# Plain cross-attention: scores in four bursts of four blocks, two of each burst copied half by ScalarE and half by VectorE

## The reference, cut to what matters

```python
q = (x @ Wq).reshape(B, N, HEADS, DIM_HEAD)        # B 2, N 256, HEADS 8, DIM_HEAD 64
k = (context @ Wk).reshape(B, M, HEADS, DIM_HEAD)  # M 4096
v = (context @ Wv).reshape(B, M, HEADS, DIM_HEAD)
sim = jnp.einsum('bihd,bjhd->bhij', q, k) * SCALE
attn = jax.nn.softmax(sim, axis=-1)
out = jnp.einsum('bhij,bjhd->bihd', attn, v).reshape(B, N, INNER)
return out @ Wo + bo
```

## Time and profile before

| | |
|---|---|
| median of three runs | 1962.62 us |
| the profiled execution: its time, its span | 1959.22 us, 1957.3 us |
| TensorE busy, of the span | 1825.8 us (93%) |
| VectorE | 1570.7 us (80%) |
| ScalarE | 857.4 us (44%) |
| GpSimd | 923.8 us (47%) |
| plain stage on TensorE | from 12.6 us to about 542 us |
| one sweep of the plain stage | 62.8 us |

### The profile page before, as it was taken

How to read it: one execution, slowest core, us unless ns; L and a number is a source line. 1 busy time by engine, 2 the same in 40 slices (tenths; PEclk the granted TensorE clock), 3 DMA queues, 4 the chain that set the end, 5 groups by cost and what they waited for, 6 DMA issues and landing times. The chain is left out here.

```text
span 1957.3 us, 44087 instructions
## 1 busy us (share of the span) xinstructions
PE 1825.8 (93%) x17242; PEld 1268.8 (65%) x17242; DVE 1570.7 (80%) x2178; ACT 857.4 (44%) x1173; POOL 923.8 (47%) x438
## 2 busy tenths in 40 slices
PE   7999999999877979899999999999999999998737
PEld 4667666667636868866666676666666666666526
DVE  4666766677777756699999999999999999999783
ACT  3666666676531135433434344334434344343401
POOL 0346655575560034116655575556655575556300
PEclk9999999999988889999999999999999999999757
DMA  3000210000030033000000000120000000000100
GB/s 137 10 15 0 66 48 13 1 12 10 7 141 1 2 149 95 29 9 2 13 13 13 8 5 13 46 68 0 13 13 13 6 7 13 13 8 1 50 0 11
DMA packets 27771, 52.77 MB, mean 27 GB/s; under 512 B 4259, under 2 KB 15284, under 8 KB 27188
## 3 DMA queue, kind: packets, MB, share of 16 engines
q1 hardware_dynamic: 27232, 51.57, 7.9%
q10 hardware_dynamic: 468, 0.16, 0.0%
HBM read 51.20 MB, written 0.52 MB: 26 GB/s over the span
## 5 line engine op out<-in xcount | busy, mean ns | idle before, releaser
L351 POOL TENSOR_TENSOR biased_sums<-biased_sums,biased_scores 128x1024 f32<-128x1024 f32 x216 | 512.4, 2372 | 138.8 <-ACT biased_scores L651 119.0
L717 DVE TENSOR_TENSOR biased_scores<-ps,bias 128x1024 f32<-128x1024 f32 x256 | 313.5, 1224 | 35.3 <-PE ps L439 33.9
L731 DVE TENSOR_TENSOR ps<-ps,biased_scores 128x512 f32<-128x512 f32 x480 | 336.5, 701 | 4.1
L738 DVE TENSOR_TENSOR biased_scores<-biased_scores,ps 128x1024 f32<-128x1024 f32 x256 | 307.5, 1221 | 3.8 <-PE ps L496 3.1
L651 ACT ACTIVATE biased_scores<-biased_scores 128x1024 f32<-128x1024 f32 x256 | 262.9, 1052 | 97.9 <-DVE biased_scores L738 95.7
L351 POOL TENSOR_TENSOR plain_sums<-plain_sums,plain_scores 128x1024 f32<-128x1024 f32 x104 | 246.5, 2370 | 60.7 <-ACT plain_scores L651 50.3
L731 DVE TENSOR_TENSOR ps<-ps,plain_scores 128x512 f32<-128x512 f32 x240 | 167.3, 697 | 118.2 <-ACT plain_scores L634 113.3
L439 PE MATMUL ps<-biased_queries,keys_again 64*128 64x256 f32 x2048 | 256.7, 390 | 3.6 <-DVE biased_scores L717 2.8
L386 PE MATMUL ps<-weights_again,context_again 128*64 128x128 f32 x4096 | 248.7, 275 | 0.0
L451 PE MATMUL ps<-biased_scores,biased_values 128*64 128x256 f32 x2048 | 245.4, 382 | 3.5 <-ACT biased_scores L651 3.2
L386 PEld LDWEIGHTS ps<-weights_again,context_again 128*64 128x64 f32 x4096 | 229.3, 138 | 28.7 <-issue 17.9
(11 more groups left out here) (407 smaller groups left out, 2238.1 us busy)
## 6 DMA issues: line engine op xcount, KB each, us to landing
moe_w<-in_moe_w SPq DMA_DIRECT2D x32, 256.0 KB, 2.7
weights_again<-in_wqkv SPq DMA_DIRECT2D x45, 128.0 KB, 2.2
context<-in_ctx_t SPq DMA_DIRECT2D x4, 1024.0 KB, 7.1
context_again<-in_ctx_t SPq DMA_DIRECT2D x4, 1024.0 KB, 7.8
bias<-in_fside SPq DMA_DIRECT2D x1, 4096.0 KB, 15.4
biased_w_out<-in_w_out SPq DMA_DIRECT2D x16, 256.0 KB, 2.6
context<-in_ctx_t SPq DMA_DIRECT2D x2, 1536.0 KB, 9.7
context_again<-in_ctx_t SPq DMA_DIRECT2D x2, 1536.0 KB, 9.7
```

Source lines behind the costliest of these rows:

```text
L351: pool.tensor_tensor(both(SUM[:, :, :, :]), both((E[:, 0] if kp == 1 else SUM)[:, :, :, :]), both(E[:, kp, :, :, :]), ALU.add).then_inc(su ...
L717: dve.tensor_tensor(E[:, kp, :, :, :].rearrange("p (h t) n j -> p h t (n j)", h=2), scores_bank(kp).rearrange("p (h t n) -> p h t n", h=2, ...
L731: ins = dve.tensor_tensor(to, highest, E[:, kp, :, n, :], ALU.max)
L738: dve.tensor_tensor(at, at, c.ps[:, LOWER, :].rearrange("p (a j) -> p a j", a=HQ).unsqueeze(2) .to_broadcast([P, HQ, 2, P]), ALU.add).then ...
```

## The change

In the plain stage a sweep that makes scores is now four bursts: W, V, W, V, then four score blocks in a row, then one K piece. Before, a pair of score blocks stood in each of the eight groups. The fourth key piece (K4) moves behind the sums at the sweep's end. In each burst the first two score blocks are copied half by ScalarE (banks of the first head) and half by VectorE (`half_out`); the other two are copied whole by ScalarE, as before. The third and fourth block of a burst wait for both halves. The biased stage keeps its order.

```diff
+BURST_PIECES = [("V", 0), ("V", 1), ("K", 0), ("V", 2), ("V", 3), ("K", 1), ("V", 4), ("V", 5), ("K", 2), ("V", 6),
+                ("V", 7), ("K", 3), ("K", 4), ("K", 5), ("K", 6), ("K", 7)]
...
+        def in_halves(kp):
+            return not biased and kp % BURST < 2
...
                     if kp >= 2:
                         pe.wait_ge(scores_kept, NP * p + kp - 1)
+                        if in_halves(kp - 2):
+                            pe.wait_ge(halves_kept, halves_count(p, kp - 2))
...
+                def bursts(m, attending):
+                    for d in range(NP // BURST):
+                        for g in (2 * d, 2 * d + 1):
+                            if attending:
+                                weigh(m, g)
+                            piece(m, ("V", g))
+                        for i in range(BURST):
+                            scores(m + 1, BURST * d + i)
+                        piece(m, ("K", d))
...
                     if more_keys:
+                        if not biased:
+                            piece(m, ("K", 4))
                         piece(m, ("K", 5))
...
+                    if in_halves(kp):
+                        act.activation(E[:, kp, 0:2, :, :].rearrange("p a n j -> p (a n j)"),
+                                       c.ps[:, 2 * (kp % 2), :], ACT.Copy).then_inc(scores_kept, 1)
...
+                def bursts(m, attending):
+                    for d in range(NP // BURST):
+                        later = range(BURST * d + AHEAD, BURST * d + AHEAD + BURST) if attending and d < NP // BURST - 1 else ()
+                        for kp in later[0:1]:
+                            exponential(m, kp)
+                        piece_out(m, ("V", 2 * d))
+                        for kp in later[1:3]:
+                            exponential(m, kp)
+                        piece_out(m, ("V", 2 * d + 1))
+                        for i in range(BURST):
+                            scores_out(m + 1, BURST * d + i, attending)
+                        piece_out(m, ("K", d))
+                        for kp in later[3:4]:
+                            exponential(m, kp)
...
+                def half_out(p, kp, attending):
+                    dve.wait_ge(scores_done, NP * p + kp + 1)
+                    if attending:
+                        dve.wait_ge(summed, NP * (p - 1) + max(kp, 1))
+                    dve.tensor_copy(E[:, kp, 2:4, :, :].rearrange("p a n j -> p (a n j)"),
+                                    c.ps[:, 2 * (kp % 2) + 1, :]).then_inc(halves_kept, 1)
...
+                def bursts(m, attending):
+                    for d in range(NP // BURST):
+                        for kp in range(BURST * d, BURST * (d + 1)):
+                            if attending and kp + AHEAD < NP:
+                                lower(m, kp + AHEAD)
+                            if d > 0:
+                                peak(m + 1, kp - BURST, 0)
+                                peak(m + 1, kp - BURST, 1)
+                        for i in range(2):
+                            half_out(m + 1, BURST * d + i, attending)
+                    for kp in range(NP - BURST, NP - 1):
+                        peak(m + 1, kp, 0)
+                        peak(m + 1, kp, 1)
```

More of the change, by code:

```diff
@@ L202, in cross_attention @@
     LAST_SUMS, LATE_SUMS = 8, 12
-    V_PIECES = [piece for piece in PIECES if piece[0] == "V"]
+    BURST = 4
+    ALL_PIECES = PIECES if biased else BURST_PIECES
+    V_PIECES = [piece for piece in ALL_PIECES if piece[0] == "V"]
     with ExitStack() as stack:
@@ L238, in cross_attention @@
         scores_done, scores_kept = sem("scores_done"), sem("scores_kept")
+        halves_kept = sem("halves_kept")
         peaked, peaks_turned, peaks_found = sem("peaked"), sem("peaks_turned"), sem("peaks_found")
@@ L257, in pieces_of @@
         def pieces_of(m):
-            return V_PIECES if isinstance(m, int) and m == END - 2 else PIECES
+            return V_PIECES if isinstance(m, int) and m == END - 2 else ALL_PIECES
         def piece_count(m, piece):
@@ L278, in piece_bank, with halves_count @@
             return PIECE_BANKS.get(which, PIECE)
+        def in_halves(kp):
+            return not biased and kp % BURST < 2
+        def halves_count(p, kp):
+            return (p - START) * (NP // BURST * 2) + kp // BURST * 2 + kp % BURST + 1
         def turn_kept(kp):
@@ L514, in project @@
                         last.then_inc(projected, 1)
+                def bursts(m, attending):
[7 more added lines that the diff above has]
+                        piece(m, ("K", d))
                 def sweep(m, attending, scoring, more_keys, batch=0):
-                    for g in range(NG):
+                    if scoring and not biased:
+                        bursts(m, attending)
+                    for g in range(NG if biased or not scoring else 0):
                         if attending:
@@ L633, in scores_out @@
                         act.wait_ge(summed, NP * (p - 1) + max(kp, 1))
-                    act.activation(both(E[:, kp, :, :, :]), scores_bank(kp), ACT.Copy).then_inc(scores_kept, 1)
+                    if in_halves(kp):
+                        act.activation(E[:, kp, 0:2, :, :].rearrange("p a n j -> p (a n j)"),
+                                       c.ps[:, 2 * (kp % 2), :], ACT.Copy).then_inc(scores_kept, 1)
+                    else:
+                        act.activation(both(E[:, kp, :, :, :]), scores_bank(kp), ACT.Copy).then_inc(scores_kept, 1)
                 def output(m):
@@ L657, in sweep @@
                                 piece_out(m, BEFORE_SCORES[g])
-                            if not biased:
-                                scores_out(m + 1, 2 * g, attending)
-                                scores_out(m + 1, 2 * g + 1, attending)
                             piece_out(m, AFTER_SCORES[g])
@@ L669, in sweep @@
                     if scoring:
+                        if not biased:
+                            piece_out(m, ("K", 4))
                         piece_out(m, ("K", 5))
@@ L724, in peak @@
                         dve.wait_ge(scores_kept, NP * p + kp + 1)
+                        if in_halves(kp):
+                            dve.wait_ge(halves_kept, halves_count(p, kp))
                     highest = c.ps[:, PEAKS, :].rearrange("p (a j) -> p a j", a=HQ)
@@ L774, in add @@
                                                  op1=ALU.add).then_inc(x_added, 1)
+                def bursts(m, attending):
[11 more added lines that the diff above has]
+                        peak(m + 1, kp, 1)
                 def sweep(m, attending, scoring):
-                    for kp in range(NP):
-                        if biased and attending and kp + AHEAD < NP:
+                    if scoring and not biased:
+                        bursts(m, attending)
+                    for kp in range(NP if biased or not scoring else 0):
+                        if attending and kp + AHEAD < NP:
                             lower(m, kp + AHEAD)
-                        if scoring and kp > 0:
-                            peak(m + 1, kp - 1, 0)
-                        if scoring and biased:
+                        if scoring:
+                            if kp > 0:
+                                peak(m + 1, kp - 1, 0)
                             scores_out(m + 1, kp, attending)
@@ L785, in sweep @@
                                 peak(m + 1, kp - 1, 1)
[L786 to L789, removed]
                     if scoring:
```

## The result

The changed kernel takes 1977.63 us (median of five runs, 1973.77 to 1980.37) against 1962.62 us (five runs, 1960.04 to 1963.25). The ratio is 1.0077, 95% interval 1.006 to 1.0093: 15 us slower, where 12.0 were forecast (1974.6 us, range 1967 to 1981). The profiled execution took 1979.72 us, its span is 1977.9 us, 20.6 longer than the span of before; the profiled execution of before (1959.22) is faster than all five of its runs, that of the changed kernel the second slowest of five, so the medians are closer together than the traces. All runs compared are fast ones.

A forecast was written before the change was run, and what follows sets the result against it. TensorE was taken as the bound, so its waits add in full: 1.9 (sweep -1) + 7.2 (sweeps 0 to 5) + 2.9 (sweep 6) = +12.0 us, giving a median of 1974.6 us, range 1967 to 1981.

The forecast's parts named there:

- a third block: Third score block of each burst waits for VectorE's half copy of the first: 0.12 late plus 0.15 restart, 0.27 us.
- K4 behind the sums: Sweeps 0 to 5: K4 uses K3's bank with only the sums between; 0.38 late, 0.5 us with the restart.
- V0 and the copy of K7: Head of a sweep: V0 shares bank 4 with K7 and waits for ScalarE's copy, 1.06 us; bounds 0.9 and 1.2.
- sweeps 0 to 5: Six steady sweeps, each -1.44 + 1.08 + 1.06 + 0.5 = +1.2 us; +7.2 us in all.
- sweep -1: First scoring sweep: VectorE's weight rounding delays the half copy, 2.7 us; with the other bursts and saved visits +1.9 us.
- sweep 6: Last scoring sweep, without K: eight peaks behind its last scores make the turning of the peaks later, +2.9 us.
- the stages behind: Stages after the plain one: start some 12 us later, clock not always full; used only to widen the range.
- The visit at 0.36: Each TensorE visit to the scores costs 0.36 us; four fewer save 1.44 us a sweep, 11.5 us in all.
- the third block did wait: Rival claim that the third block of a burst hardly waits: total +3.8 us, 1966.4 us; chance 13%.
- VectorE was not the bound: Rival claim that VectorE becomes the bound, each burst's half late by 0.4 to 0.8 us: about 1990 us; chance 7%.
- the faster case: Rival claim that ScalarE and VectorE free the banks before TensorE asks: -3.5 us, 1959.1 us; chance 8%.

The follow-up runs named there:

- 7: Changed kernel with all score blocks copied whole by ScalarE, VectorE copying none: 1983.49 us (two runs), ratio 1.0115 to the kernel before.
- 5: Changed kernel with K4 through bank 1 and K5 through bank 4 from sweep 0 on: 1973.57 us (four runs), ratio 1.0062 to the kernel before.
- 1: Changed kernel with the values' weights asked for ahead of those of queries and keys: 1976.12 us (three runs), ratio 1.0084 to the kernel before.
- 6: Changed kernel with values' weights first, V0 and K4 each in bank 1, rounding early: 1961.70 us (ten runs) against 1960.68 before, ratio 1.0004.
- 4: Changed kernel with the later stage's weights rounded as soon as they are loaded: 1970.93 us (two runs), ratio 1.0051 to the kernel before.
- 9: Kernel of 6, with sweep 6 in the order and whole copies of before: 1958.96 us (eleven runs) against 1962.03 before, ratio 0.9988.
- 8: Kernel before the change, started later by 16 tile fillings on VectorE ahead of the first stage: 1970.03 us (four runs), ratio 1.0047.
- experiment 3: Changed kernel with the rounding of the later stage's weights behind the first two half copies of sweep -1: 1978.78 us, ratio 1.0096 to the kernel before.

## Why the forecast was right, and where it was short

The sign, the range and the cause were right: four visits less in a sweep were more than paid back by new waits for copies. The size was nearer than the working earned. The forecast's 12.0 us were all in the plain stage, which lost 16.4 in the traces (562.61 - 546.25); the medians differ by 15.0. Term by term, from the traces:

| | forecast | changed kernel | shown by |
|---|---|---|---|
| a third block | +0.27 | +0.30 (3.94 to 3.95 against 3.65) | 7 |
| K4 behind the sums | +0.5 | +0.43 | 5 |
| V0 and the copy of K7 | +1.06 | +1.03 | 1 |
| sweeps 0 to 5 | +7.2 | +9.4 | 1, 6 |
| sweep -1 | +1.9 | +4.1 | 4 |
| sweep 6 | +2.9 | +3.55: 2.55 to the turning, 1.0 behind it | 9; not the 1.0 |
| the stages behind | about 0 | +4.2 | 8: not needed by the change; cause open |

The visit at 0.36 fits as well: with the waits gone, 62.57 us is what it and the third block leave. Only the sum of the two was measured there; the third block has its own rows, 0.30.

Short by one term was "V0 at the head of a sweep": I had followed the bank and ScalarE, but not the queue that fetches V0's weights, though V0 had been moved ahead in time and its transfer had not. Experiment 1 gives the size, 1.9 us over six sweeps. The upper bound that I gave for this step, 1.2 us, was too low: it reached 1.6 (W0 to V0 3.33 in sweep 5, less 1.72 for W0).

"Sweep -1" was right in its wait (2.6 us seen) and short in what the wait does: the clock fell behind it, some 1.65 us more. In sweep 6 the peaks came 2.55 us later (2.9 forecast). Another 1.0 was lost between the turning and the next sweep, 8.58 us (528.88 - 520.30) instead of 7.58 (512.15 - 504.57), with a mean clock there of 0.67 against 0.77. That 1.0 is not tied to the bursts: experiment 1 keeps them and lacks it (57.83), experiment 9 has the old order and has it. "The stages behind" I had put into the range alone, and there they belong: the same instructions there took 278.9 to 283.7 us.

The traces add up: -0.35 (the work ahead of sweep -1's scores) + 4.1 + 9.4 + 3.55 - 0.4 (sweep 7) + 4.0 (delta rule and experts) + 0.2 (the stages behind them) = 20.5 us, the 20.6 between the spans to rounding. The medians are 15 us apart. The difference of 5.6 lies in which executions were profiled, 3.4 under its median before and 2.1 over it after; which stages it sits in is open, since the other runs have no trace.

The rivals: the third block did wait, VectorE was not the bound (1.45 us idle ahead of its halves), and the faster case needed exactly what experiment 6 had to build: banks and transfers that are ready in time. Even then the gain is 0.23 us in a sweep, because the third block takes back most of it, and the time of experiment 6 is that of the kernel before.

## What to carry to other kernels

When a step is moved ahead, write down everything it waits for, each with the time it becomes ready, transfers and their place in the queue too: here two waits ended within 0.6 us of each other, and taking away either alone gave 0.3 us a sweep or nothing, where both stand for 1.0 to 1.6. Gathering work of one form saves its edges; with two pairs of banks for a burst of four blocks, each burst paid 0.30 us for a copy (no run here had more banks). In sweep -1 a wait of 2.6 us cost 1.65 us more than itself, since the clock fell behind it. And before a difference of a few us is put down to a change, compare the stages that it did not touch.

## What was not expected of the hardware

A single wait of 2.62 us in sweep -1 was followed by stretches with a mean granted clock of 0.72 and 0.64; without the wait (experiments 4 and 7) it stayed at 1.00, and when the wait moved to the second burst the low stretch moved there (0.53, experiment 3). And two stages that no edit touched took 278.9 to 283.7 us over eleven traces, in no order of their starts.
